# A graph layer on one core: a reordered opening, and 64-column one-hots over two halves of each edge group

## The reference, cut to what matters

```
xn  = layernorm(x)
# graph part, the part that the change is about
e   = edge_attr @ W_edge + b_edge                 # 50000 x 256
msg = relu(xn[src] + e)
agg = segment_sum(msg, dst)                       # 3125 x 256, dst sorted
h   = relu(((1+eps)*xn + agg) @ W1 + b1) @ W2 + b2
gnn = relu(batchnorm(h))
# linear attention over all nodes, 8 heads of 32
q, k, v = elu(xn Wq')+1, elu(xn Wk')+1, xn Wv'
mix = (q (k'v)) / (q sum k) @ Wproj' + bproj
x   = x + gnn + mix
# top-2 of 8 experts, 256 -> 1024 -> 256 with exact gelu
return x + ffn(layernorm(x))
```

## Time and profile before

| | |
|---|---|
| median of 3 runs (range) | 1177.69 us (1177.09 to 1181.65) |
| span of the profiled execution, first to last instruction | 1050.8 us |
| time of that execution outside its span | not given; the median less the span is 126.9 us |
| instructions | 17977 |
| PE, DVE, POOL, ACT busy, share of the span | 92%, 64%, 53%, 49% |
| mean granted TensorE clock | 0.967 of full speed |

### The profile page before, as it was taken

The page is one execution under the profiler, slowest core; times in us unless marked ns, Lnnn a source line. Parts: engine busy times, 40 slices in busy tenths (PEclk is TensorE's granted clock), DMA queues, the critical chain, the costliest instruction groups (busy, mean ns, idle before and its releaser), DMA issues.

```text
span 1050.8 us, 17977 instructions
## 1 busy us (share of the span) xinstructions
PE 964.7 (92%) x5112; PEld 810.3 (77%) x5113; DVE 671.7 (64%) x1274; ACT 513.5 (49%) x1036; POOL 555.1 (53%) x627
## 2 busy tenths in 40 slices
PE   5898999999999999999998961799999999999994
PEld 4677888888888888877775860778888888888884
DVE  5455565656655565578886778666666666666663
ACT  3644555555454545455554566444444444444442
POOL 3277777777777777777760040224253353444442
PEclk8899999999999999999998986899999999999998
DMA  9667788788888878998762028412545636635321
GB/s 246 197 154 237 255 267 253 250 268 266 260 254 262 269 247 267 278 313 270 239 202 86 26 89 316 181 26 40 204 90 174 220 50 213 192 73 160 98 38 21
DMA packets 85472, 198.30 MB, mean 189 GB/s; under 512 B 19785, under 2 KB 37139, under 8 KB 84378
## 3 DMA queue, kind: packets, MB, share of 16 engines
q1 hardware_dynamic: 55926, 131.60, 36.1%
q0 software_dynamic: 28752, 64.45, 25.5%
q10 hardware_dynamic: 724, 1.42, 0.5%
HBM read 147.86 MB, written 49.97 MB: 188 GB/s over the span
## 4 chain that ended last, share of the span: by engine, by line
POOL 29%; PE 29%; DMA 19%; issue 13%; DVE 7%; ACT 2%; POOLq 1%; SPq 0%; DVEq 0%; ACTq 0%
POOL work L758 29%; DMA out<-work,rowc 11%; PE banks L1141 6%; PE banks L1166 4%; DMA work<-token_table,tokc 4%; PE banks L470 3%; PE banks L446 3%; PE banks L1168 2%; PE banks L969 2%; PE banks L1054 2%; PE banks L1151 2%; DMA work<-in_edge_attr 1%; PE banks L1042 1%; DMA wts<-in_src 1%; DVE st L1776 1%
## 5 line engine op out<-in xcount | busy, mean ns | idle before, releaser
L758 POOL DMA_INDIRECT work<-node_table,srcT x391 | 379.5, 971 | 157.0 <-issue 117.6
L470 PE MATMUL banks<-work 128*128 128x256 f32 x780 | 179.1, 379 | 1.1 <-issue 1.1
L446 PE MATMUL banks<-w_edge,eaT 128*128 128x256 f32 x780 | 179.3, 380 | 0.0
L470 PEld LDWEIGHTS banks<-work 128*128 128x128 f32 x780 | 148.0, 190 | 21.8 <-issue 1.8
L446 PEld LDWEIGHTS banks<-w_edge,eaT 128*128 128x128 f32 x780 | 143.4, 191 | 16.8
L1166 PE MATMUL banks<-wsplit,hidT_hi 128*128 x416 | 153.3, 408 | 2.1 <-DVE hidT_lo L1908 2.1
L529 DVE TENSOR_TENSOR work<-banks,work 128x512 f32<-128x512 f32 x195 | 126.8, 682 | 26.1 <-DMA work<-node_table,srcT 15.2
L1141 PE MATMUL banks<-wsplit,xeT_hi 128*128 x416 | 134.3, 404 | 2.8 <-DVE xeT_lo L1915 2.8
L483 ACT COPY wts<-banks 128x256 f32<-128x256 f32 x66 | 24.6, 372 | 228.8 <-PE banks L470 227.8
L811 POOL DMA_INDIRECT out<-work,rowc x52 | 83.4, 1605 | 82.2 <-ACT work L1441 45.6
L1168 PE MATMUL banks<-wsplit,hidT_lo 128*128 x416 | 116.8, 281 | 0.0
(11 more groups left out here) (263 smaller groups left out, 1555.2 us busy)
## 6 DMA issues: line engine op xcount, KB each, us to landing
wsplit<-split_table SPq DMA_DIRECT2D x8, 4096.0 KB, 15.3
work<-in_edge_attr SPq DMA_DIRECT2D x65, 384.0 KB, 4.6
wts<-in_L_ffn_W SPq DMA_DIRECT2D x64, 256.0 KB, 4.9
split_table<-raw_hi SPq DMA_DIRECT2D x64, 256.0 KB, 3.0
split_table<-raw_lo SPq DMA_DIRECT2D x64, 256.0 KB, 4.3
work<-node_table,srcT POOLq DMA_INDIRECT x391, 4.2
xs<-in_x SPq DMA_DIRECT2D x8, 560.0 KB
wts<-in_L_ffn_b SPq DMA_DIRECT2D x8, 512.0 KB, 4.0
```

Source lines behind the costliest of these rows:

```text
L446: last = nc.tensor.matmul(b[:, k * DIM:(k + 1) * DIM], eaT[:, u, 2 * q + k], w_edge[:], start=True, stop=True)
L470: last = nc.tensor.matmul(bank[5][:, 0:DIM], onehot[:, u, j], msg[:, u, j], start=(j == 0), stop=(j == GT - 1))
L758: pool.indirect_dma_start(out=xg[n % NB][0:rows, j], out_offset=None, in_=node_table, in_offset=bass.IndirectOffsetOnAxis(ap=srcT[0:rows, ...
```

## The change: what it does

In the opening: ACT's queue loads chunks 1 and 2 of `x` first, SP's 0, 3 and 4; the mixer's and MLP's weights are issued on SP after the table rows; the ACT table for the square root is loaded before it is needed; the statistics go in four rounds (chunks 0, 1, 2, then 3 and 4) whose small steps POOL does; POOL adds `b_edge` for chunks 0 to 2, DVE for 4 and 3; DVE normalises chunk 4; POOL sets `hT` to zero after that. DVE makes the router's constant (`wc`), the `dst` tables and `relT` after its share of this; PE's second transpose (chunk 1) waits for `wc_ready`. The mixer's weights are turned in iteration 0 of the edge loop, after `miss_known`, and DVE's first mark waits for them (they lie where one-hots and messages go).

In the loop: a group's 768 edges are taken as two halves of 384 consecutive ones, each with its own least target. The one-hots have 64 columns, the six matmuls go in turn to partitions 0 to 63 and 64 to 127 of bank 5, and `add_window` becomes `add_first` and `add_second`, one ahead of the mark of the group and one after it. An attribute load has two pieces of 1536 bytes per partition in place of one of 3072.

```diff
-WINDOW = P
+WINDOW = P // 2
-LEAD = ((0,), (1, 2), (3, 4))
+ROUNDS = ((0, 1), (1, 2), (2, 3), (3, 5))
+BY_POOL = 3
...
-            rows = a["edge_attr_128"][bass.ds(g * GROUP, GROUP), :].rearrange("(p j) d -> p (j d)", j=GT)
+            rows = a["edge_attr_128"][bass.ds(g * GROUP, GROUP), :].rearrange("(s p j) d -> p s (j d)", s=2, j=PAIRS)
...
+        def in_half(i):
+            return (i % 2) * PAIRS + i // 2
...
             for j in range(GT):
                 if j % 2 == 0:
                     pe.wait_ge(msg_ready, PAIRS * n + j // 2 + 1)
-                last = nc.tensor.matmul(bank[5][:, 0:DIM], onehot[:, u, j], msg[:, u, j], start=(j == 0), stop=(j == GT - 1))
+                half = slice(j % 2 * WINDOW, (j % 2 + 1) * WINDOW)
+                last = nc.tensor.matmul(bank[5][half, 0:DIM], onehot[:, u, j], msg[:, u, j], start=(j < 2), stop=(j >= GT - 2))
             last.then_inc(agg_ready, 1)
...
         def mark_from_psum(dve, g, u):
             dve.wait_ge(mx_ctx, g // 2)
-            nc.vector.tensor_tensor(onehot[:, u], numbers.unsqueeze(1).to_broadcast([P, GT, P]),
-                                    relT[:, g].unsqueeze(2).to_broadcast([P, GT, P]), ALU.is_equal).then_inc(onehot_ready, 1)
+            wide = [P, GT, WINDOW]
+            nc.vector.tensor_tensor(onehot[:, u], numbers.unsqueeze(1).to_broadcast(wide),
+                                    relT[:, g].unsqueeze(2).to_broadcast(wide), ALU.is_equal).then_inc(onehot_ready, 1)
...
+        turned = bank[5][:, DIM:2 * DIM].rearrange("p (h s c) -> p s h c", h=HALVES, s=2)
-        def add_window(dve, n, start, mixed, fresh=False):
+        def add_first(dve, n, start, mixed, fresh=False):
...
             w = hT[:, :, bass.ds(start, WINDOW)]
+            nc.vector.tensor_tensor(w, turned[:, 0], w, ALU.add).then_inc(agg_first, 1)
...
+        def add_second(dve, n, start):
+            dve.wait_ge(agg_first, n + 1)
+            w = hT[:, :, bass.ds(start, WINDOW)]
+            nc.vector.tensor_tensor(w, turned[:, 1], w, ALU.add).then_inc(agg_read, 1)
...
 # SyncE
-            load_x(2)
+            load_x(3)
             load_x(4)
-            weights = [ ... seven loads ... ]
             load_edges(sp, 0, 0, 0, True)
-            load_edges(sp, 1, 1, 1, True)
...
+            for c, ready, n in ((0, rows_pool, 1), (1, rows_pool, 2), (4, rows_dve, 1), (2, rows_pool, 3), (3, rows_dve, 2)):
+                sp.wait_ge(ready, n)
+                for d, s in node_rows(node_table, table_stage[c], c):
+                    sp.dma_start(d, s).then_inc(rows_stored, 16)
+            sp.dma_start(w_natural[:, 2:6], ... Wkv ...)
+            load_edges(sp, 1, 1, 1, True)
+            ... Wq, Wproj, W1, W2
+            sp.wait_ge(rows_stored, 32 * CHUNKS)
             for i in range(RAWS):
                 load_raw(sp, i)
...
 # GpSimd
+            for r in range(3):
+                moments(r)          # seven small tensor operations, each waited for
+            add_bias(0)
+            moments(3)
+            for c in range(1, BY_POOL):
+                add_bias(c)
             nc.gpsimd.memset(hT[:], 0.0).then_inc(h_zero, 1)
...
 # TensorE
+                if c == 1:
+                    pe.wait_ge(wc_ready, 1)
+                    pe.wait_ge(tables_ready, 2)
...
             x_transpose(0)
+            x_transpose(1)
             x_route(0)
-            x_transpose(1)
             x_transpose(2)
             x_route(1)
-            ... turn the weights ...
             x_transpose(3)
             x_route(2)
             x_transpose(4)
             x_route(3)
+            pe.wait_ge(xT_copied, 3 * (CHUNKS - 1))
+            pe.wait_ge(rel_ready, 2)
+            ... turn the two rows of least targets and rel: nine transposes ...
+            def turn_weights():
+                pe.wait_ge(weights_in, WEIGHT_DMAS * 16)
+                pe.wait_ge(miss_known, 1)
+                ... eight transposes ... .then_inc(wT_ready, 1)
+                pe.wait_ge(wT_copied, 2)
+                ... eight transposes ... .then_inc(wT_ready, 1)
+                pe.wait_ge(wT_copied, 4)
...
 # ScalarE
-            normalise_x(0, LEAD[0])
+            for r in range(3):
+                normalise_x(r)
             copy_xT(0)
-            ... rounds 1 and 2, each with a copy_xT ...
+            normalise_x(3)
+            for c in range(1, CHUNKS):
+                copy_xT(c)
...
 # VectorE
+            stats_of(0).then_inc(stats_ready, 1)
+            scale_of(0)
+            stats_of(1).then_inc(stats_ready, 1)
+            stats_of(2).then_inc(stats_ready, 1)
+            dve.wait_ge(ids_in, 64)
+            nc.vector.tensor_copy(src_f, src_i).then_inc(rel_ready, 1)
+            scale_of(1)
+            stats_of(3)
+            scale_of(2)
+            stats_of(4).then_inc(stats_ready, 1)
+            ... srcT ...
+            scale_of(3)
+            normalise_x(4)
+            dve.wait_ge(small_in, SMALL_DMAS * 16)
+            add_bias(4)
+            add_bias(3)
+            ... wc, then the dst tables, relT, base_row, the spans
...
                 if n >= 2:
-                    add_window(dve, n - 2, starts[(n - 2) % GT], mixed_by(n + 1), n == 2)
+                    add_first(dve, n - 2, starts[2 * ((n - 2) % GT)], mixed_by(n + 1), n == 2)
                 if n >= 2:
                     dve.wait_ge(agg_ready, n - 1)
+                if n == 0:
+                    dve.wait_ge(wT_ready, 2)
...
+                if n >= 2:
+                    add_second(dve, n - 2, starts[2 * ((n - 2) % GT) + 1])
```

More of the change, by code:

```diff
@@ L47 @@
 PAIRS = GT // 2
+HALF = GROUP // 2
 PIECES = 4
@@ L256, in build @@
         eaT_out = pair01[:, :, 0:3 * P]
-        numbers = bank[7][:, 3 * P:4 * P]
+        numbers = bank[7][:, 3 * P:3 * P + WINDOW]
         x_in = [sem(f"x_in{c}") for c in range(CHUNKS)]
@@ L283, in build @@
         xn_ready = sem("xn_ready")
-        rows_ready = sem("rows_ready")
-        rows_stored = [sem(f"rows_stored{i}") for i in range(STAGES)]
+        xn_last = sem("xn_last")
+        rows_pool = sem("rows_pool")
+        rows_dve = sem("rows_dve")
+        rows_stored = sem("rows_stored")
         ids_memset = sem("ids_memset")
@@ L434, in transpose_edges @@
             for j in range(tiles):
-                last = nc.tensor.transpose(bank[j // 3][:, (j % 3) * P:(j % 3 + 1) * P], ea[:, u, j], ident[:])
+                last = nc.tensor.transpose(bank[j // 3][:, (j % 3) * P:(j % 3 + 1) * P], ea[:, u, in_half(j)], ident[:])
             return last
@@ L459, in aggregate_tail @@
             pe.wait_ge(msg_ready, PAIRS * (n + 1))
-            nc.tensor.matmul(bank[5][:, 0:DIM], onehot[:, u, 0], msg[:, u, 0], start=True, stop=True).then_inc(agg_ready, 1)
+            for i in range(2):
+                last = nc.tensor.matmul(bank[5][i * WINDOW:(i + 1) * WINDOW, 0:DIM], onehot[:, u, i], msg[:, u, 0],
+                                        start=True, stop=True)
+            last.then_inc(agg_ready, 1)
         def aggregate(pe, n, u, fresh=False):
@@ L469, in aggregate, with aggregate_pass @@
                     pe.wait_ge(msg_ready, PAIRS * n + j // 2 + 1)
-                last = nc.tensor.matmul(bank[5][:, 0:DIM], onehot[:, u, j], msg[:, u, j], start=(j == 0), stop=(j == GT - 1))
+                half = slice(j % 2 * WINDOW, (j % 2 + 1) * WINDOW)
+                last = nc.tensor.matmul(bank[5][half, 0:DIM], onehot[:, u, j], msg[:, u, j], start=(j < 2), stop=(j >= GT - 2))
+            last.then_inc(agg_ready, 1)
+        def aggregate_pass(pe, n):
+            pe.wait_ge(agg_copied, n)
+            pe.wait_ge(agg_read, n)
+            pe.wait_ge(onehot_ready, n + 1)
+            pe.wait_ge(msg_ready, PAIRS * (n + 1))
+            for j in range(GT):
+                last = nc.tensor.matmul(bank[5][:, 0:DIM], onehot_pass[:, j], msg[:, 0, j], start=(j == 0), stop=(j == GT - 1))
             last.then_inc(agg_ready, 1)
@@ L851, in x_transpose @@
                         o = ((k % 2) * HALVES + h) * TILE
-                        last = nc.tensor.transpose(bank[k // 2][:, o:o + TILE],
+                        last = nc.tensor.transpose(bank[3 * (c % 2) + k // 2][:, o:o + TILE],
                                                    xs[0:TILE, c * CHUNK_TILES + k, h * P:(h + 1) * P], ident[0:TILE, 0:TILE])
@@ L987, in _ @@
                     pe.wait_ge(top_ready, 1)
[L988 removed]
+                    nc.tensor.transpose(bank[6][0:1, 0:GROUPS], gstat[:, TOP], ident[0:GROUPS, 0:GROUPS]).then_inc(top_T, 1)
+                    turn_weights()
                 if n == DEN0:
@@ L1298, in copy_group, with copy_weights @@
                     copy_tail(act, n, n % 2)
+            def copy_weights():
+                act.wait_ge(wT_ready, 1)
+                for k in range(2):
+                    nc.scalar.copy(wkvT[:, k], bank[5 + k][:]).then_inc(wT_copied, 1)
+                act.wait_ge(wT_ready, 2)
+                for t, b in ((wqT, 5), (wpT, 6)):
```

(12 more changed lines are left out.)

267 lines of the change are left out of this document (148 added, 119 removed).

## The result

The changed kernel took 1210.45 us (median of 4, 1199.29 to 1215.0) against 1177.39 us (4 runs) for the kernel before: ratio 1.0275 [1.0204, 1.0345]. In a second series, both together on one chip: 1.034 [1.0264, 1.0417]. The change is 33 to 38 us slower, where 8 us faster was forecast.

A forecast was written before the change was run, and what follows sets the result against it. PE and POOL's gathers were taken as equal bounds at 7.6 us a group, POOL setting the pace; opening +1.1, groups 51 on -4.0, after the last gather -5 gave -8: 1177.7 - 8 = 1170 us, range 1160 to 1188.

The forecast's parts named there:

- the 126.9 us between median and span: Whole program: time beyond the profiled span of 1050.8 us, kept unchanged and added to the predicted span of 1043.
- The opening's +1.1: Opening: first gather six us earlier, but group 2 starts at 61.1 and not 59.99, so 1.1 us slower.
- Groups 2 to 50: PE 6.5, POOL 7.6.: Edge loop before the attention: PE falls to 6.5 us a group, POOL's 7.6 sets the pace, so change 0.
- Groups 51 on: -4.0: Edge loop with attention: PE falls from 8.3 to 7.2 us a group, three of POOL's four waits go, -4.0 us.
- After the last gather: -5: Loop's end: PE no longer comes 5 to 7 us behind the last gather, -5 us, between -2 and -7.
- `wc`: 31 us.: Opening: DVE makes the router's constant at 31 us, after normalising chunk 4 and two bias sums; PE's second transpose waits.
- the 2 to 4 named for them: Opening: if DVE's bias sums each wait for a POOL sum, the opening comes 2 to 4 us later.
- Group 0's sums end at about 60.8.: Opening's end: group 0's sums, which group 2's gathers need, end at about 60.8 us in place of 56.15.
- seven steps of twelve: 1.5: Loop's aggregation on PE: six matmuls in alternating halves overlap partly, 1.5 us, 1.1 us off PE per group.
- the rival without overlap: Loop: halves don't overlap and switching costs 0.2 us a group over 65 groups, +13, giving 1191 us; chance 0.15.
- POOL's seven small steps, taken at 1.9: Opening: POOL's seven small statistics steps of a round take 1.9 us, between bounds of 1.2 and 2.8.
- The clock falls: Rival, loop: PE, idle 1.1 us a group, loses full clock every few groups, +5 on the forecast, 1175; chance 0.08.

The follow-up runs named there:

- The memset experiment: Changed kernel with DVE making `wc` right behind the last statistics and POOL's `hT` memset back at its start: 1199.73 us, ratio 1.0131 to the kernel before.
- the plain copies' new loop: Kernel with the old opening and new loop, plain copies of table rows in place of gathers: 1040.09 us, with 56 slots run and not 52.
- three fillers: Kernel with only the new loop, plus three filler matmuls on PE ahead of each aggregation: 1208.69 us, ratio 1.0174 to the kernel before.
- the rows' execution: Profiled execution of the unchanged kernel before that the prediction was read from: span 1050.8 us, while its times lie at 1177.
- six fillers: Kernel with only the new loop, plus six matmuls of ones on PE ahead of each aggregation: 1266.89 us, ratio 1.0672 to the kernel before.

## Why the prediction was wrong, step by step

- **"The page gives no time of the profiled execution outside its span, so I keep the 126.9 us between median and span": this failed, and the three terms of the loop (0, -4.0, -5) with it.** The opening's +1.1 failed by itself (below). The difference was inside the loop: 632.6 us in a timed execution, 505.1 in the one shown. 127 us, a quarter of a 505 us loop, outside a span that starts with the first instruction was not credible, and the prediction should have made a rival of it: the execution shown is not like those timed. In those neither engine is full (PE 199.89 and POOL 141.97 of 240 us), and "the time is POOL's: 0" was asked of a loop that no timed execution has. What came in its place is a loop 16 to 23 us longer.
- **"Groups 2 to 50: PE 6.5, POOL 7.6."** Both figures are right as work (PE 6.66 where it is the bound, with plain copies). The pace between groups 2 and 50 is 9.84 us a group before, 10.01 after and 10.12 with only the new loop: two groups of gathers in a burst, then a wait until a landing releases PE's semaphores and DVE makes up to three sums.
- **"Groups 51 on: -4.0" and "After the last gather: -5".** From group 50's start to 64's 9.58 us a group before, 10.36 after; from the last gather to `edges_done` 17.9 before and 17.5 after. -0.4 and not -5.
- **"`wc`: 31 us."** It came at 41.66. ACT's copy 0, ahead of the last square root, ended at 28.8 and not 25.4 (PE waited to 19.45 for the small loads): +3.4. DVE's scale step of 0.17 took 2.82 beside POOL's bias sums: +2.7. The normalisation of 1.5 took 6.74 beside POOL's memset: +5.2, all of it in the first of its five instructions, which took 5.45 us where the other four took 0.40. (In the second trace of this kernel the scale step took 0.17 and that first instruction 8.28: the wait falls on one or the other and ends with the memset either way.) The prediction named such an overlap as a danger, for DVE's bias sums, and left it out of the sum. The bias sums were not held, 1.49 and 1.48 us, for POOL was done by then; that +2.7 lies inside the 2 to 4 named for them is luck. The rule of the Trainium skill ("SBUF — State Buffer", Who interferes with whom) is about any DVE instruction with two inputs in SBUF beside a GpSimd one that reads SBUF, and the trace agrees with it at the scale steps, 1.85 and 2.82 and not 0.17. The same section of the Trainium skill says that a `tensor_scalar` in a two-port mode contends with GpSimd. The memset experiment, 6.74 against 1.70, fits that; in which mode these ran, no row shows.
- **"Group 0's sums end at about 60.8."** They ended at 78.89. From `wc` on 37.2 us and not 29.8: the copy of group 0's attributes was held for 7.0 us, and the embedding behind it ran mostly at half clock, 4.24 and not 2.75. This and `wc` are the opening's miss: +19.2 us at group 2 against before, and not +1.1.
- **Right:** the steps on single instructions, in 150 to 450 us after (busy, mean ns | idle before):

```profile
L550 DVE TENSOR_TENSOR work<-banks,relT 128x384 f32<-128x384 f32 x30 | 16.4, 547 | 0.0
...
L580 DVE TENSOR_TENSOR hT<-banks,hT 128x128 f32 x30 | 8.7, 290 | 77.9 <-remote 62.5 <-PE banks L507 13.1 <-issue 2.3
```

  Mark 0.55, adds 0.29 and 0.28; and the six matmuls of 64 columns in 1.51 us at full clock, by the timeline of the plain copies' new loop:

```profile
205.79 1.51 PE L484 MATMUL banks<-work 128*64 128x256 f32 x12
```

  The halves do overlap, as "seven steps of twelve: 1.5" had it, and the rival without overlap is out. (Six full ones take 2.75 and not the 2.59 taken from the chain of the earlier trace rows, so the saving is 1.24 and not 1.1.) POOL's seven small steps, taken at 1.9, took 1.94.
- **The rivals.** "The clock falls" saw half clock behind idle time, at 5 us. The clock did fall (0.934 to 0.909), but three fillers raised it to 0.93 with no gain that shows, so it goes with the loss and isn't shown to cause it. None of the rivals held the mechanism that decided.

Open: why the rows' execution has no hold-ups and all timed ones have, and whether the recording of events plays a part; why the halves lose under hold-ups, which is argued and not shown; whether gathering itself matters or only a gapless stream from POOL's queue (long plain streams weren't tried); how the 12 us beside PE's part divide; and why six fillers cost 62 us. No version here beats the kernel before; plain copies do, but compute something else.

## What to carry to other kernels

Compare the span of the trace you reason from with the times you are to predict, before anything else: where they differ by more than a few us, find an execution like the timed ones. In a loop whose waits end in held semaphores, less work on an engine need not be a gain, and here it was a loss; ask what releases the wait, and test that alone (plain copies in place of gathers cost one line). In an opening, place the tiny instructions that a long chain hangs on before the long ones behind which they would wait: two of about 0.2 us set group 2 by 14 us.

## What the runs showed of the hardware that I had not expected

- In the timed executions, while POOL issued gathers without a gap (1.25 us apart, for 12 in a row), PE's semaphores came up to 18 us late and in bunches 0.06 to 0.09 us apart; those of DVE, ACT and POOL did not. With a gap of a landing behind each group the longest was 5.4 us; with plain copies, none. In the rows' execution of the same program none was late beside 500 us of such gathers.
- Traces with hold-ups hold 7500 to 8600 semaphore events, those without 16451 to 17102.
- A third of the loop's bytes less (204 to 142 GB/s) changed nothing of it that shows: ratio 0.9964, held 441 and not 438 us.
- A DVE `scalar_tensor_tensor` on 5 to 10 columns took 1.85 and 2.82 us and not 0.17 beside a POOL sum with two inputs; POOL's sums took 2.9 us each, near the 2.63 of the earlier trace rows.
- Five `tensor_scalar` on DVE beside a POOL memset of 5.43 us took 6.74 us and not 1.70: the first waited until the memset had ended, 5.45 us, the others took 0.40 each.
- Six fp32 matmuls of 64 stationary columns in turn to two halves of the array took 1.51 us, against 2.75 for six of 128.
